# Gather and scatter by one-hot matmuls: the stationaries of line 717 take 125 columns instead of 128

## The chip, the cores and the metric

One core of a Trainium2 chip runs the kernel. The metric is device time in microseconds, the median of several executions: 469.66 us before the change, over 3 runs (468.04 to 470.31). One more execution was recorded by the hardware profiler; all rows of the trace are from that one.

## The reference

A block of a graph network on 1250 nodes with 512 features and 20000 edges. Everything is fp32.

```
xn  = layernorm(x)
gnn = relu(segsum((relu(segsum((xn @ W1.T + b1)[src], dst)) @ W2.T + b2)[src], dst))
q   = softmax(xn @ Wq.T, axis=-1) / sqrt(512);  k = softmax(xn @ Wk.T, axis=-2);  v = xn @ Wv.T
a   = q @ (k.T @ v) + xn
mix = a @ mW1.T @ mW2.T + a
x   = x + gnn + mix
x   = x + moe(layernorm(x))     # gates by 8 sinkhorn rounds, top 156 tokens for each of 8 experts
```

Here segsum(m, dst) adds the rows of m that have the same target node. The change lies in how this sum is prepared. The sum over edges is a product with the matrix A of edge counts: A[source, target] is how many edges lead from that source to that target. The kernel counts A once and uses it in both layers as a dense product.

## The kernel before

**Tiles.** The 1250 nodes are 10 tiles of 125 (TT = 125). The 512 features are 4 blocks of 128. The fp32 products are made of three terms, high by high, low by high and high by low part, and all are written by terms(), whose matmul is line 732: 12 matmuls of up to 512 columns for a tile, each with its own weight load.

**Counting the edges.** The edges are sorted by target and cut into 160 tiles of 125 edges (ET = 125). The targets are cut into 125 blocks of 8 to 11 (WIDTHS), and a visit is one pair of a block and an edge tile that may have edges into it: 322 visits in all. A visit is one matmul (line 717). Its stationary is a mark of 125 edges by 128 columns, with a 1 in the column that is the place of the source node within its tile of 125; its moving operand is a mark of 125 edges by 10 times the width of the block (80 to 110 columns), with a 1 in the column for the target and the tile of the source. The product adds the edge into the counts in a bank of PSUM, of which 125 rows are nodes.

**Who makes the marks.** VectorE makes both marks for four visits at a time (BATCH = 4): line 1683 the moving ones (RING_D, MARK_D), line 1685 the stationary ones (RING_S, MARK_S), the latter with 128 columns for each visit by comparing with every_home, which counts 0 to 127. A place in a tile is at most 124, so columns 125 to 127 hold only zeros. It then raises `marked`. The marks stand in a ring of 5 sets (2 sets at first), and a set is written again when `visited` says that TensorE has used it.

**Where the visits run.** They are put between the matmuls of other products. visits_in_products() gives each group of four visits a place: in the products vp, cp, q, x and h, six fp32 matmuls apart, or twelve in the products h. terms() calls visits() in front of its n-th matmul. The order on TensorE is so written out by hand; there is no scheduler. The first visit of a group waits for `marked`, and the last raises `visited`. When all visits into a bank are done, ScalarE copies 125 rows of it to AT (line 1300) and raises `adj_hi`, and the bank, one of two, is free for the next group of blocks.

**Other 16-bit products.** The rows further down also show lines 829 and 834 (a product of f16 stationaries of 125 columns, with 322 columns moving, between the fp32 matmuls of line 845), lines 1089 and 1090 (two bf16 stationaries of 125 columns, with 80 columns moving) and line 1039 (fp32 matmuls that fill waits of TensorE).

Of the kernel before, what the change touches and what calls it, by code (L numbers as in the profile page):

```python
# [33 lines left out]
TT = 125  # L34
# [11 lines left out]
BATCH = 4  # L46
# [178 lines left out]
def ring_slot(k):  # L225


    return k % RING_A if k < IN_A else RING_A + (k - IN_A) % RING_B
# [10 lines left out]
def gps_block(nc, x_in, src_t, dst_t, rows_in, gW1T, gb1, gW2T, gb2, WqT, WkT, Wv, mW1, mW2T,  # L239
# [5 lines left out]
    with ExitStack() as ctx:  # L245
# [170 lines left out]
        PS = [PSUM[:, 512 * b:512 * (b + 1)] for b in range(8)]  # L416

        def view(name, chunks=C):
            return PS[plan[name][0]].rearrange("p (c t) -> p c t", c=chunks)
# [50 lines left out]
        def hot_s(k):  # L470

            r = ring_slot(k)
            return MARK_S[0:ET, r] if r < RING_A else RING_S[0:ET, r - RING_A]

        def hot_d(k, w):

            r = ring_slot(k)
            return MARK_D[0:ET, r, :, 0:w] if r < RING_A else RING_D[0:ET, r - RING_A, :, 0:w]

        def width(b):  # L480

            return NT * WIDTHS[b]

        def group(g):

            lo, hi = GROUPS_OF_TARGETS[g]
            return EDGES[lo], EDGES[hi]
# [206 lines left out]
        def _(pe):  # L694
            def opens(name):

                for what, value in plan[name][2]:
                    pe.wait_ge(done[what], value)
                return PS[plan[name][0]]
# [4 lines left out]
            def visits(unit, n):  # L704

                for v in VISITS_AT.get((unit, n), ()):
                    b, s = ORDER[v]
                    g, k = GROUP_OF[b], v // BATCH
                    if s == 0 and b == GROUPS_OF_TARGETS[g][0]:
                        if g < 2:  # L710
                            opens(f"adj{4 + g}")
                        else:
                            pe.wait_ge(done["adj_hi"], g - 1)
                    if v % BATCH == 0:
                        pe.wait_ge(done["marked"], k + 1)
                    o = NT * (EDGES[b] - group(g)[0])
                    mm = pe.matmul(PS[4 + g % 2][:, o:o + width(b)], hot_s(k)[:, v % BATCH, :], hot_d(k, width(b))[:, v % BATCH, :],  # L717
                                   start=(s == 0), stop=(s == VISITS[b] - 1), skip_group_check=True)
                    if v % BATCH == BATCH - 1 or v == NV - 1:
                        mm.then_inc(done["visited"], 1)  # L720

            def terms(ps, stationary, moving, first=True, last=True, between=None, at=1, before=None, unit=None, base=0):

                pairs = [(a, b, c) for c in range(C) for a, b in ((0, 0), (0, 1), (1, 0))]
                for n, (a, b, c) in enumerate(pairs):
                    if n == at and between is not None:
                        between()
                    if n or not base:
                        visits(unit, base + n)
                    if n % 3 == 0 and before is not None:  # L730
                        before(c)
                    mm = pe.matmul(ps, stationary[a](c), moving[b](c), start=(first and n == 0), stop=(last and n == len(pairs) - 1))  # L732
                return mm
# [42 lines left out]
            for c in range(C):  # L776
                mm = pe.matmul(ps[0:TT, 0:NE], ones[:, 0:TT], gw1[:, c, :], start=(c == 0), stop=(c == C - 1))
# [18 lines left out]
            for c in range(C):  # L796
# [9 lines left out]
                if c == 0:  # L806
                    pe.wait_ge(done["kmax_step"], NT)
                    opens("kmt")
                    for f in range(C):
                        mm = pe.transpose(view("kmt")[:, f, 0:TT], KMAX[0:TT, 128 * f:128 * (f + 1)], ident[0:TT, 0:TT])  # L810
# [52 lines left out]
            for c in range(C):  # L863
                product(f"vp{c}", opens(f"vp{c}")[:], (block_of(WVH, c), block_of(WVL, c)), (rows_of(MPH), rows_of(MPL)),
                        unit=f"vp{c}")
                if c == 0:
                    pe.wait_ge(done["esum_step"], NT)
                    ps = opens("ks")
                    for f in range(C):
                        mm = pe.matmul(ps[:, f:f + 1], ESUM[0:TT, 128 * f:128 * (f + 1)], ones[0:TT, 0:1], start=True, stop=True)  # L870
# [9 lines left out]
            def mix(i):  # L880

                ps = opens(f"xq{i}")[0:TT, :]
                terms(ps, (tile_of(XTH, i), tile_of(XTL, i)), (rows_of(MPH), rows_of(MPL)), last=False, unit=f"x{i}")
                visits(f"x{i}", 12)
                pe.wait_ge(done["qtl_ready"], i + 1)
                if i == 0:
                    pe.wait_ge(done["cpl_ready"], C)
                    pe.wait_ge(done["cph_ready"], C)
                product(f"xq{i}", ps, (tile_of(QTH, i % 2), tile_of(QTL, i % 2)), (rows_of(CPH), rows_of(CPL)), first=False,
                        unit=f"x{i}", base=12)  # L890
# [53 lines left out]
            for ch, (c0, c1) in enumerate(CHUNKS):  # L944
                def place(f):
                    return PS[plan[f"z{ch}_{f}"][0]][:, 0:c1 - c0]
# [10 lines left out]
                with pe.If(large[0] > 0):  # L957
                    for k in range(NT):
                        pe.wait_ge(done["ac_ready"], ch * NT + k + 1)
                        for f in range(C):  # L960
                            for h in (H1H, H1L):
                                mm = pe.matmul(place(f), h[0:TT, k, 128 * f:128 * (f + 1)], AC[0:TT, k % 2, 0:c1 - c0], start=False, stop=False)
# [3 lines left out]
                for f in range(C):  # L966
                    k = NT - 1
# [97 lines left out]
            for name, lo, hi in (("key_a", 0, DVE_T), ("key_b", DVE_T, (DVE_T + NT) // 2), ("key_c", (DVE_T + NT) // 2, NT)):  # L1065
                ps = opens(name)
                for i in range(lo, hi):
                    if i % 4 == 0:
                        pe.wait_ge(done["p_ready"], SINKHORN + 1 + i // 4)
                    mm = pe.transpose(ps[:, TT * (i - lo):TT * (i - lo + 1)], WIDE[i // 4][0:TT, i % 4].rearrange("p e l -> p (e l)"),  # L1070
                                      ident[0:TT, 0:TT])
                closes(name, mm)
            for r in range(ROUNDS):
                ps = opens(f"rad{r}")
                p = NHI * (r // NHI)
                for n in range(p, r + 1):
                    if n == r:
                        pe.wait_ge(done["ind_ready"], r + 1)
                    mm = pe.matmul(ps[:, 0:1], same[:].rearrange("p e l -> p (e l)"), marks[:, n:n + 1], start=(n == p), stop=(n == r))
# [19 lines left out]
            for i in range(NT):  # L1099
# [3 lines left out]
                mm = pe.matmul(ps[0:SLOT, 0:NC], RS[h][0:TT, :, i - lo], PLACE[0:TT, :, i], start=(i == 0), stop=(i == NT - 1))  # L1103
# [4 lines left out]
            for i in range(NT):  # L1108
                h, lo = (0, 0) if i < MASKED[0][1] else (1, MASKED[1][0])
                mm = pe.matmul(ps[0:SLOT, 0:3 * NC], RS[h][0:TT, :, i - lo], GATE[0:TT, :, :, i], start=(i == 0), stop=(i == NT - 1))  # L1110
# [974 lines left out]
```

## Time and profile before

| | |
|---|---|
| median of 3 runs | 469.66 us (468.04 to 470.31) |
| the profiled execution | 469.05 us, of which the span from first to last instruction 467.3 us |
| TensorE matmuls busy | 449.9 us, 96% of the span, 2449 instructions |
| TensorE weight loads busy | 349.5 us, 75% |
| VectorE / ScalarE / GpSimd busy | 312.4 / 150.6 / 64.0 us |
| granted clock of TensorE, mean | 0.994 |
| visits (line 717) | 322, first at 87.5 us, last at 233.6 us |

PE is TensorE's matmul row, PEld its row of weight loads, DVE VectorE, ACT ScalarE. Matmuls are pipelined: the record of one begins when it is issued and ends when its last result has been written, by a model. So the records of neighbours overlap, and the time that a matmul costs is read from the distance of its start to the next start. Shapes stand as contraction*stationary columns, then the moving operand: `125*128 125x110 bf16` is a stationary of 125 rows and 128 columns and 110 moving columns.

### The profile page before, as it was taken

The numbers are of one execution on the slowest core, as the hardware profiler recorded it, in microseconds if no ns is written. First come the engines' busy times: TensorE is split into PE (matmuls) and PEld (weight loads), VectorE is DVE, ScalarE is ACT, GpSimd is POOL, SyncE is SP. The second block draws the span as 40 slices with busy tenths as digits, with TensorE's granted clock in tenths as the row PEclk, the third lists the DMA queues.
The fourth block names the chain that finished last, engine by engine and source line by source line (L and its number), as shares of the span: only waits on it lengthen the run. The fifth ranks groups of instructions, "written<-read, shape, count | busy, mean of one in ns | idle before, by whom it ended". The sixth has DMA issues, their size and how long they took to land.

```text
span 467.3 us, 6438 instructions
## 1 busy us (share of the span) xinstructions
PE 449.9 (96%) x2449; PEld 349.5 (75%) x2449; DVE 312.4 (67%) x681; ACT 150.6 (32%) x274; POOL 64.0 (14%) x108
## 2 busy tenths in 40 slices
PE   8999999999999999999999999999999999778995
PEld 4788778777777777777779999777777776454783
DVE  5995799899987888887741110444546567777972
ACT  4686454332322323242222111222141116441110
POOL 3188210000000000000004000004100000005642
PEclk9999999999999999999999999999999989999998
DMA  7902002912000000002100000004744459106791
GB/s 214 283 9 90 1 0 63 239 16 93 14 1 0 2 0 1 1 1 85 41 1 2 1 1 3 0 0 126 241 135 130 140 163 391 62 1 229 255 350 71
DMA packets 20824, 40.42 MB, mean 87 GB/s; under 512 B 2936, under 2 KB 3266, under 8 KB 20787
## 3 DMA queue, kind: packets, MB, share of 16 engines
q1 hardware_dynamic: 18547, 32.55, 22.4%
q0 software_dynamic: 2240, 7.39, 4.3%
q8 instruction: 23, 0.38, 0.3%
q14 instruction: 14, 0.11, 0.1%
HBM read 30.10 MB, written 10.30 MB: 86 GB/s over the span
## 4 chain that ended last, share of the span: by engine, by line
PE 85%; DVE 8%; ACT 3%; DMA 1%; issue 1%; SPq 1%; POOLq 0%; DVEq 0%; ACTq 0%
PE ps L732 47%; PE ps L1022 9%; PE ps L954 9%; PE ps L845 5%; PE ps L717 3%; PE ps L1039 2%; ACT scrap_a L1397 2%; PE ps L1148 2%; DMA RAW_K<-in_WkT 1%; PE ps L1118 1%; PE ps L877 1%; PE ps L981 1%; PE ps L766 1%; PE ps L1061 1%; PE ps L1003 1%
## 5 line engine op out<-in xcount | busy, mean ns | idle before, releaser
L1685 DVE TENSOR_TENSOR RING_S<-every_home,HOME 125x512 bf16<-125x512 f16 x64 | 43.8, 684 | 0.0
L954 PE MATMUL ps<-AT,H1H 125*128 125x416 f32 (+1 forms) x108 | 38.0, 352 | 0.0
L954 PE MATMUL ps<-AT,H1L 125*128 125x416 f32 (+1 forms) x108 | 38.0, 351 | 0.0
L1683 DVE TENSOR_TENSOR RING_D<-places,PLACES 125x440 bf16<-125x440 f16 (+3 forms) x64 | 36.4, 569 | 0.0
L1022 PE MATMUL ps<-H2H,AT 125*125 125x512 f32 x90 | 36.1, 402 | 0.0
L1022 PE MATMUL ps<-H2L,AT 125*125 125x512 f32 x90 | 35.5, 394 | 0.0
L1039 PE MATMUL ps<-WE0H 128*128 128x512 f32 x125 | 35.4, 419 | 0.0
L1753 DVE TENSOR_TENSOR ps<-ps,bias 125x512 f32<-125x512 f32 x20 | 14.0, 700 | 28.7 <-PE ps L732 28.7
L1834 DVE SCALAR_TENSOR_TENSOR ZL<-ps,ZH 128x416 fp32r<-128x416 f32 (+1 forms) x12 | 6.3, 584 | 38.7 <-ACT ZH L1350 38.7
L606 POOL TENSOR_TENSOR G2L<-RAW_G,G2H 128x512 fp32r<-128x512 f32 x4 | 5.0, 1299 | 188.4 <-ACT G2H L1167 188.4
L1039 PEld LDWEIGHTS ps<-WE0H 128*128 128x128 f32 x125 | 22.8, 197 | 3.7
L717 PEld LDWEIGHTS ps<-RING_D,RING_S 125*128 125x128 bf16 x254 | 14.0, 99 | 15.1 <-issue 10.5
L677 POOL DMA_INDIRECT YX<-scratch,idx x10 | 11.8, 1181 | 95.6 <-DVE idx L1990 92.9
L717 PE MATMUL ps<-RING_D,RING_S 125*128 125x110 bf16 (+3 forms) x254 | 22.6, 211 | 0.0
L1300 ACT ACTIVATE AT<-ps 125x440 fp32r<-125x440 f32 (+7 forms) x28 | 15.3, 545 | 18.7 <-PE ps L717 18.7
L954 PEld LDWEIGHTS ps<-AT,H1H 125*128 125x128 f32 x108 | 20.3, 188 | 0.2
L954 PEld LDWEIGHTS ps<-AT,H1L 125*128 125x128 f32 x108 | 20.3, 188 | 0.3
L1884 DVE SCALAR_TENSOR_TENSOR X<-ps,X 125x512 f32<-125x512 f32 x10 | 6.9, 692 | 19.7 <-PE ps L1034 19.7
L1022 PEld LDWEIGHTS ps<-H2H,AT 125*125 125x125 f32 x90 | 16.7, 186 | 4.0 <-issue 0.2
L1022 PEld LDWEIGHTS ps<-H2L,AT 125*125 125x125 f32 x90 | 16.7, 185 | 3.8
L732 PE MATMUL ps<-CPH,QTH 128*125 128x512 f32 x40 | 17.4, 435 | 0.0
L732 PE MATMUL ps<-WQH,XTH 128*125 128x512 f32 x40 | 17.4, 435 | 0.0
(401 smaller groups left out, 1175.6 us busy)
## 6 DMA issues: line engine op xcount, KB each, us to landing
RAW_E<-in_experts SPq DMA_DIRECT2D x8, 1024.0 KB, 9.2
RAW_AGAIN<-in_experts SPq DMA_DIRECT2D x3, 1024.0 KB, 8.8
X<-in_x SPq DMA_DIRECT2D x1, 2240.0 KB
out_x<-X SPq DMA_DIRECT2D x10, 224.0 KB
scratch<-X SPq DMA_DIRECT2D x10, 224.0 KB
scratch<-Y SPq DMA_DIRECT2D x10, 224.0 KB
RAW_K<-in_WkT SPq DMA_DIRECT2D x4, 256.0 KB, 5.1
RAW<-in_mW2T SPq DMA_DIRECT2D x1, 1024.0 KB, 12.8
```

What stands on the lines that cost most here:

```text
L677: nc.gpsimd.indirect_dma_start(out=YX[0:SLOT, j % RING].rearrange("p a f -> p (a f)"), out_offset=None, in_=scratch, in_offset=bass.Indire ...
L717: mm = pe.matmul(PS[4 + g % 2][:, o:o + width(b)], hot_s(k)[:, v % BATCH, :], hot_d(k, width(b))[:, v % BATCH, :], start=(s == 0), stop=(s ...
L732: mm = pe.matmul(ps, stationary[a](c), moving[b](c), start=(first and n == 0), stop=(last and n == len(pairs) - 1))
L845: mm = pe.matmul(ps[:], x[0:TT, i, f], e[0:TT, i % 4, :], start=(i == 0 and n == 0), stop=(i == NT - 1 and n == 2))
L954: pe.matmul(place(f), h[0:TT, k, 128 * f:128 * (f + 1)], AT[0:TT, k, c0:c1], start=(k == 0 and n == 0), stop=False)
L1022: pe.matmul(ps, AT[0:TT, k, t], h[0:TT, k, :], start=(k == 0 and n == 0), stop=False)
L1039: pe.matmul(PS[bank][:], WEH[0][:, 0, 0:128], WEH[0][:, 0, :], start=True, stop=True)
L1148: mm = pe.matmul(ps[p, 0:hi - lo], FTR[:, c, p], raw[q][:, c, lo:hi], start=(c == 0), stop=(c == C - 1), skip_group_check=True)
L1300: nc.scalar.activation(AT[0:TT, :, lo:hi], counts_of(g), ACT.Copy).then_inc(done["adj_hi"], 1)
L1683: V.tensor_tensor(hot_d(k, w), places[0:ET, 0:w].unsqueeze(1).broadcast_to([ET, BATCH, w]), PLACES[0:ET, c].unsqueeze(2).broadcast_to([ET, ...
L1685: V.tensor_tensor(hot_s(k), every_home[0:ET].unsqueeze(1).broadcast_to([ET, BATCH, 128]), HOME[0:ET, c].unsqueeze(2).broadcast_to([ET, BAT ...
L1753: V.tensor_tensor(ps, ps, bias[layer - 1][0:TT, :], ALU.add).then_inc(done["h1_biased" if layer == 1 else "h2_biased"], 1)
```

## The change

The stationary operand of each visit is cut to its first 125 columns, and the result goes to the first 125 rows of the bank. Only the slices in this one call are different.

```diff
-                    mm = pe.matmul(PS[4 + g % 2][:, o:o + width(b)], hot_s(k)[:, v % BATCH, :], hot_d(k, width(b))[:, v % BATCH, :],
+                    mm = pe.matmul(PS[4 + g % 2][0:TT, o:o + width(b)], hot_s(k)[:, v % BATCH, 0:TT], hot_d(k, width(b))[:, v % BATCH, :],
                                    start=(s == 0), stop=(s == VISITS[b] - 1), skip_group_check=True)
```

VectorE still makes marks of 128 columns, and no instruction is added, taken out or moved on any engine: 322 weight loads and 322 matmuls stand where they stood. The loads are of 125 columns, the matmuls write 125 rows, and the moving operand, the waits and the semaphores are the same. The columns that are left out held zeros, and the rows that are no longer written were not read.

## Rows read from the trace of the kernel before

**Rows 1.** windows: us; busy us (count) of each engine; granted clock, DMA share, GB/s.

```profile
85.00:235.00 150.00, 150.00 (x904) 111.99 (x903) 126.61 (x231) 47.33 (x91) 0.00 (x0) 1.00 0.12 35
```

**Rows 2.** chain of waits, 85 to 240 us: share by line.

```profile
by line: PE ps L732 85.7%; PE ps L717 10.3%; PE ps L877 2.8%; PE ps L845 0.9%; PE ps L870 0.5%
```

**Rows 3.** visits by shape: count, busy us, mean ns, idle before.

```profile
L717 PE MATMUL ps<-RING_D,RING_S 125*128 125x110 bf16 x140 | 13.6, 215 | 0.0
L717 PE MATMUL ps<-MARK_D,MARK_S 125*128 125x110 bf16 x49 | 4.7, 215 | 0.0
L717 PE MATMUL ps<-RING_D,RING_S 125*128 125x90 bf16 x48 | 4.3, 207 | 0.0
L717 PE MATMUL ps<-RING_D,RING_S 125*128 125x80 bf16 x46 | 3.9, 203 | 0.0
L717 PE MATMUL ps<-RING_D,RING_S 125*128 125x100 bf16 x20 | 1.9, 210 | 0.0
L717 PE MATMUL ps<-MARK_D,MARK_S 125*128 125x100 bf16 x12 | 1.2, 209 | 0.0
```

**Rows 4.** timeline of PE, one group of visits: start us, us.

```profile
128.15 0.40 PE L732 MATMUL ps<-WQH,XTL 128*125 128x512 f32 x1
128.39 0.38 PE L717 MATMUL ps<-RING_D,RING_S 125*128 125x110 bf16 x4
128.58 0.48 PE L732 MATMUL ps<-WQH,XTH 128*125 128x512 f32 x1
128.90 0.40 PE L732 MATMUL ps<-WQL,XTH 128*125 128x512 f32 x1
```

**Rows 5.** timeline of weight loads at the same place.

```profile
128.38 0.22 PEld L717 LDWEIGHTS ps<-RING_D,RING_S 125*128 125x128 bf16 x4 [0.28 <-issue]
128.55 0.19 PEld L732 LDWEIGHTS ps<-WQH,XTH 128*125 128x125 f32 x1
128.66 0.19 PEld L732 LDWEIGHTS ps<-WQL,XTH 128*125 128x125 f32 x1
```

**Rows 6.** line 717, first visit of that group alone: min/median/max ns.

```profile
L717 PE MATMUL ps<-RING_D,RING_S x1: 223/223/223, 128.4 to 128.4; 125*128 125x110 bf16 x1
```

**Rows 7.** line 717, all: min/median/max ns; idle us, times before its loads.

```profile
L717 PEld LDWEIGHTS ps<-RING_D,RING_S x254: 95/98/111, 116.5 to 233.6; 125*128 125x128 bf16 x127
L717 PE MATMUL ps<-RING_D,RING_S x254: 197/212/226, 116.5 to 233.6; 125*128 125x110 bf16 x70, 125*128 125x90 bf16 x24, 125*128 125x80 bf16 x23, 125*128 125x100 bf16 x10
  issue: 14.8, 54
  DVE RING_S L1685: 4.5, 16
```

**Rows 8.** timeline of PE, groups of 100 and 80 columns.

```profile
98.22 0.35 PE L717 MATMUL ps<-MARK_D,MARK_S 125*128 125x100 bf16 x4
...
158.02 0.32 PE L717 MATMUL ps<-RING_D,RING_S 125*128 125x80 bf16 x4
```

**Rows 9.** timeline, 16-bit stationaries of 125 columns back to back.

```profile
415.95 0.13 PEld L1089 LDWEIGHTS ps<-before,ones 125*125 125x125 bf16 x1 [1.04 <-DVE before L1947]
415.95 0.25 PE L1089 MATMUL ps<-before,ones 125*125 125x80 bf16 x1 [0.61 <-DVE before L1947]
416.00 0.14 PEld L1090 LDWEIGHTS ps<-equal,tri 125*125 125x125 bf16 x1
416.03 0.23 PE L1090 MATMUL ps<-equal,tri 125*125 125x80 bf16 x1
416.06 0.19 PEld L1039 LDWEIGHTS ps<-WE0H 128*128 128x128 f32 x1
```

**Rows 10.** timeline, a 16-bit 125-column load behind an fp32 product.

```profile
76.55 0.39 PE L845 MATMUL ps<-EH,XNL 125*128 125x512 f32 x1
76.78 0.44 PE L829 MATMUL ps<-SEL,keys 80*125 80x322 f16 x2
...
76.55 0.36 PEld L829 LDWEIGHTS ps<-SEL,keys 80*125 80x125 f16 x2
```

## The prediction

> **What bounds the kernel now.** [...] The chain of waits over the same stretch consists of TensorE alone: 85.7% is line 732, the fp32 products, and 10.3% line 717, the visits [rows 2]. No other engine ends a wait in it. Time that a visit gains or loses is therefore gained or lost by the kernel, almost one for one: nothing in this stage has slack to take it, and what comes after starts from it.
>
> A busy matmul row says nothing of how close together the matmuls run, since records overlap: 322 visits with records of some 0.21 us [rows 3, 7] would be 68 us one after the other, and the chain gives them 10.3% of 155, 16 us. What counts is the distance from one start to the next. In a group of four visits of 110 columns [rows 4] the last fp32 matmul starts at 128.15, the visits at 128.39, the fp32 product goes on at 128.58, its second matmul starts at 128.90. The weight loads of the same place are the second view [rows 5]: four loads of 128 bf16 columns from 128.38, then the fp32 loads at 128.55 and 128.66.
>
> Two things are to be seen there. First, the first visit's load does not run under the fp32 matmul before it: the load engine stands for 0.28 us ("issue") and starts only 0.01 before the visit itself. This happens in front of 54 + 16 = 70 groups [rows 7]; 16 name VectorE's marks, but the distance is the same, so I count them alike (the other 11 of the 81 groups have no such idle before them). The visit then waits in the array for its weights, and its record shows it: 0.223 us [rows 6] against a median of 0.212 [rows 7], 0.011 late. Second, the other loads are hidden under the visit before them.
>
> **What changes.** 322 weight loads take 125 bf16 columns instead of 128; the instructions and their order, the moving columns, every wait, VectorE's marks and ScalarE's copies stay as they are. The copies read 125 rows before and after. So three terms are possible: how long a load takes, how close visits follow each other, and what the first load of a group costs.
>
> *The load itself.* A load of 128 bf16 columns has a record of 0.098 us [rows 7]. The trace has 16-bit loads of 125 columns too: 0.13 and 0.14 for bf16 [rows 9]. Three columns fewer, yet 0.037 longer. [...] Loads hold the path only where they are not hidden, so the 0.037 is not simply multiplied by 322.
>
> *Distance between visits.* Now: a group of four of 110 columns spans 0.38 us [rows 4]; less the last record (0.212) and the 0.011 by which the first is late, 0.157 for three distances, 0.052 each. 100 columns: 0.35 less 0.207 and 0.011, 0.044. 80 columns: 0.32 less 0.200 and 0.011, 0.036 [rows 8]. The records of the shapes are the means [rows 3] less the first visits' share of the lateness. 90 columns I put between, at 0.040. The distance follows the columns, so the moving data set it, not the load. With 125 columns the load may set it. Its pace is seen where such loads stand back to back [rows 9]: loads at 415.95, 416.00 and 416.06, 0.055 apart, with matmuls of 80 columns between them. I take 0.056 for every shape. Ends: 0.050, the shorter of the two distances there, and 0.060, the longer. The shapes count 189 of 110 columns, 32 of 100, 46 of 80 [rows 3] and the remaining 55 of 90; three in four have a visit behind them in their group. Added: 142 x 0.004 + 24 x 0.012 + 41 x 0.016 + 34.5 x 0.020 = 0.57 + 0.29 + 0.66 + 0.69 = 2.2 us. With 0.050 (110 columns stay at their own 0.052) it is 1.0, with 0.060 3.2.
>
> *First load of a group.* Here the change may even help. A 16-bit load of 125 columns behind an fp32 matmul stands in [rows 10]: it starts at 76.55 together with that matmul, and the 16-bit matmul follows at 76.78, 0.23 later, with its weights in place. The fast load of the visits never does that behind an fp32 product of line 732: all 70 stand back. If the ordinary load is the one that may go early, a first visit starts streaming 0.23 after the last fp32 matmul, where now it takes 0.24 + 0.011. Read to 0.01, that saves 0.01 to 0.02; I take 0.017, in 70 groups 1.2 us (ends 0.7 and 1.4). It needs the marks 0.23 earlier; if the 16 groups that name VectorE cannot have them, they lose 0.04 each instead and the term shrinks to about 0.3.
>
> *Last visit to fp32.* The fp32 load starts with the last visit and takes 0.11 (128.55 to 128.66) [rows 5], before as after: nothing. [...]
>
> Sum: +2.2 - 1.2 = +1.0 us, ends -0.4 (1.0 - 1.4) and +2.9 (3.2 - 0.3). The profiled execution took 469.05 us (its span 467.3), so 470.1 by itself; the median of the three runs before is 469.66, 0.6 higher, and the forecast for a median is **470.7 us**.
>
> **Rivals.**
>
> *A: the first load stays behind the fp32 matmul.* Place: the step from line 732 to line 717, 70 times. For: all 70 stand back now, and the kind of matmul in flight could be the reason rather than the kind of load; the one place of the other sort [rows 10] has 80 rows and f16. Against: that place has the same fp32 matmul in front. Price: the load is exposed in full. The first matmul and its load start together and its record is 0.25 instead of 0.20 [rows 9], 0.053 late rather than 0.011; 70 x 0.042 = 2.9 more and no 1.2 saved: +2.2 + 2.9 = +5.1, 474.8 us. Each group that stays back moves the sum by 0.042 + 0.017, so from 1.0 us it passes 2.35 at 23 of the 70 groups; below that the answer is still no change.
>
> *B: the ordinary load is as slow as an fp32 load.* fp32 loads of 125 columns are 0.11 apart where they bind [rows 5]. Distance 0.11: 142 x 0.058 + 24 x 0.066 + 41 x 0.070 + 34.5 x 0.074 = 15.3, less 1.2: +14.1, 483.8 us. Against it: 0.055 [rows 9], and records of 0.13 to 0.14 for 16-bit against 0.19 for fp32. [...]
>
> *C: faster.* The first load goes under the fp32 matmul and the distance stays with the moving columns: -1.2, 468.5 us. It decides when the distance for 110 columns stays at 0.052 and the others stay under it by their present margin. Against: 0.055 with only 80 columns moving.
>
> *D: nothing happens.* The load is made as before although three columns are left out, so 469.7. Against: 0.13 and 0.14 for 125 bf16 columns in this very program.
>
> **Chances and range.** Forecast 58%, A 24%, B 4%, C 7%, D 7%. What can be told from no change here is about 0.5%, 2.35 us: below 467.3 or above 472.0. Slower takes A, B and the uppermost part of the forecast's own spread (72.6 less 72.0 at its end), 5%: 33%. Faster: C stays within the 2.35, only the scatter of the runs (468.04 to 470.31) could carry it over: 5%. The rest, 62%, is no change. The range must reach A, since A alone is a quarter: low 468.6 (C), high 475.4 (A with its distance at 0.058).
>
> **What would show it.** Loads of line 717 with a record of 0.13 to 0.14 (else D). The four matmuls of a group at equal distances, 0.055 to 0.057, whatever their columns. The "issue" idle of 14.8 us before the loads gone and the first visit's load starting with the fp32 matmul before it; if it is still there and the first records are some 0.25 to 0.26 us, A is right. A distance of 0.1 would be B. Prediction and sum fail together if time moves outside 85 to 235 us.

## The result and the profile after

| | before | after |
|---|---|---|
| median (22 runs each) | 468.25 us (467.11 to 470.31) | 469.64 us (468.51 to 473.56) |
| ratio after / before | | 1.0034, 95% interval 1.0019 to 1.0049 |
| profiled execution | 469.05 us, span 467.3 | 472.16 us, span 470.4 |

The kernel became slower by a third of a per cent, 1.6 us (0.9 to 2.3). That is small and still clear of zero. Behind it are two effects of opposite sign, one of them larger than the sum and the other nearly as large.

The stretch from 85 to 235 us is filled by TensorE as before [rows 1, 2]: first the windows view (busy time and count of PE, PEld, DVE, ACT, POOL, then clock, DMA share, GB/s), then the shares of the chain of waits by line.

```profile
85.00:235.00 150.00, 150.00 (x898) 122.08 (x898) 126.60 (x232) 46.99 (x90) 0.00 (x0) 1.00 0.13 36
```

```profile
by line: PE ps L732 83.1%; PE ps L717 11.6%; PE ps L877 2.8%; PE ps L845 2.1%; PE ps L870 0.5%; PE ps L860 0.1%
```

The load row is busy for 122.08 us instead of 111.99, and the visits hold 11.6% of the chain instead of 10.3%. All loads of line 717 have a median record of 0.138 us now, against 0.098 [rows 7] (below, a load with the short record is called fast, one with the long record ordinary), and the list of what ended the idle time before them, which named "issue" 54 times and the marks 16 times, is empty:

```profile
L717 PEld LDWEIGHTS ps<-RING_D,RING_S x254: 134/138/139, 118.5 to 236.7; 125*125 125x125 bf16 x127
L717 PE MATMUL ps<-RING_D,RING_S x254: 199/222/242, 118.8 to 236.8; 125*125 125x110 bf16 x70, 125*125 125x90 bf16 x24, 125*125 125x80 bf16 x23, 125*125 125x100 bf16 x10
its engine sat idle before it (us, times) until:
who waited for it (us, times):
```

A group of 110 columns in the timeline of matmuls, and below it one of 80, to be held against [rows 4, 8]:

```profile
149.90 0.39 PE L732 MATMUL ps<-CPH,QTL 128*125 128x512 f32 x1
150.13 0.39 PE L717 MATMUL ps<-RING_D,RING_S 125*125 125x110 bf16 x4
150.33 0.47 PE L732 MATMUL ps<-WQH,XTH 128*125 128x512 f32 x1
150.64 0.39 PE L732 MATMUL ps<-WQL,XTH 128*125 128x512 f32 x1
...
160.58 0.37 PE L717 MATMUL ps<-RING_D,RING_S 125*125 125x80 bf16 x4
```

and its weight loads, against [rows 5]:

```profile
149.90 0.48 PEld L717 LDWEIGHTS ps<-RING_D,RING_S 125*125 125x125 bf16 x4
150.31 0.19 PEld L732 LDWEIGHTS ps<-WQH,XTH 128*125 128x125 f32 x1
150.41 0.19 PEld L732 LDWEIGHTS ps<-WQL,XTH 128*125 128x125 f32 x1
```

The first load of the group starts at 149.90, together with the fp32 matmul before it; in [rows 5] it started 0.01 before its own matmul. The first visit follows 0.23 after the fp32 matmul with its weights in place. In exchange the group is longer: 0.39 less a record of 0.212 leaves 0.178 for three distances, 0.059 each (0.052 before), and with 80 columns 0.37 less 0.200 leaves 0.17, 0.057 each (0.036 before). The distance no longer follows the moving columns, with 0.059 and 0.057 for 110 and 80 of them; that the load sets it is the reading that the experiments try.

Now the same over all groups. A visit whose load started only 0.01 before it has a longer record (0.223 us for the first visit of [rows 6] against the 0.212 of an undisturbed one), so what its record is longer than an undisturbed one of its shape is added to its start. The 241 distances inside groups then sum to 11.19 us before and 14.07 after (0.0464 and 0.0584 on average; after, visits of 80, 90, 100 and 110 columns all stand 0.058 behind one of their own shape), +2.9 us. From the fp32 matmul to the streaming of the first visit, the 70 places behind a product of line 732 take 0.248 us each before and 0.230 after, together -1.3 us. The visits begin and end here, in the kernel before and after:

```profile
87.53 0.38 PE L717 MATMUL ps<-MARK_D,MARK_S 125*128 125x110 bf16 x4
...
233.54 0.27 PE L717 MATMUL ps<-RING_D,RING_S 125*128 125x110 bf16 x2
```

```profile
89.44 0.39 PE L717 MATMUL ps<-MARK_D,MARK_S 125*125 125x110 bf16 x4
...
236.74 0.26 PE L717 MATMUL ps<-RING_D,RING_S 125*125 125x110 bf16 x2
```

146.01 us from the first group to the last before, 147.30 after: +1.29 us, 1.0028 of the whole, inside the measured interval. (The two effects give +1.6; the rest of the stretch came out 0.3 shorter, 0.2 of it in the step from the last visit of a group to the fp32 product.) But the visits also begin 1.9 us later, at 89.44. The windows view of the first 20 us, before and then after, shows one difference: the mean granted clock is 1.00 and 0.91 (0.50 in the stretch from 11 to 14 us of the kernel after).

```profile
0.00:20.00 20.00, 17.34 (x75) 10.99 (x76) 14.19 (x38) 10.33 (x19) 6.11 (x37) 1.00 0.91 228
```

```profile
0.00:20.00 20.00, 16.32 (x64) 10.61 (x65) 12.69 (x36) 8.63 (x17) 6.12 (x37) 0.91 0.91 237
```

Ahead of it, TensorE waited for the DMA transfer of the gate weights, in the timelines before and after:

```profile
8.04 1.04 PE L777 MATMUL ps<-gw,onesr 128*125 128x8 f32 x8 [0.24 <-DMA gw<-in_gate]
```

```profile
9.31 1.04 PE L777 MATMUL ps<-gw,onesr 128*125 128x8 f32 x8 [1.61 <-DMA gw<-in_gate]
...
11.92 0.63 PE L732 MATMUL ps<-WKL,XTH 128*125 128x512 f32 x1
```

The wait was 1.61 instead of 0.24 us, and then the fp32 matmuls ran for a while at a granted clock of 0.50, with records of 0.63 instead of 0.39 and starts 0.43 apart instead of 0.23. All this lies over 75 us ahead of the first changed instruction. Whether it belongs to the change is asked below.

### The profile page after: what moved, and what is told of

Same layout as the page of the kernel before. It is cut to its first block, busy times and chain, and to the rows that moved or that the text cites. A ratio compares the mean times of both kernels' runs of the same rounds, so it can differ in the third digit from the quotient of the medians.

```text
span 470.4 us, 6438 instructions
## 1 busy us (share of the span) xinstructions
PE 452.0 (96%) x2449; PEld 361.8 (77%) x2449; DVE 312.3 (66%) x681; ACT 150.6 (32%) x274; POOL 64.1 (14%) x108
## 4 chain that ended last, share of the span: by engine, by line
PE 86%; DVE 7%; ACT 3%; issue 1%; DMA 1%; SPq 1%; POOLq 0%; DVEq 0%; ACTq 0%
PE ps L732 47%; PE ps L1022 9%; PE ps L954 9%; PE ps L845 5%; PE ps L717 4%; PE ps L1039 2%; ACT scrap_a L1397 2%; PE ps L1148 2%; DMA gw<-in_gate 1%; PE ps L1118 1%; PE ps L877 1%; PE ps L766 1%; PE ps L981 1%; PE ps L1061 1%; PE ps L1003 1%
## 5 line engine op out<-in xcount | busy, mean ns | idle before, releaser
L717 PEld LDWEIGHTS ps<-RING_D,RING_S 125*125 125x125 bf16 x254 | 24.4, 137 | 7.6
L717 PE MATMUL ps<-RING_D,RING_S 125*125 125x110 bf16 (+3 forms) x254 | 24.4, 220 | 0.0
L732 PE MATMUL ps<-MPH,XTH 128*125 128x512 f32 x40 | 17.4, 435 | 0.0
```

What stands on the lines that cost most here:

```text
L717: mm = pe.matmul(PS[4 + g % 2][0:TT, o:o + width(b)], hot_s(k)[:, v % BATCH, 0:TT], hot_d(k, width(b))[:, v % BATCH, :], start=(s == 0), s ...
```

## The experiments

The theory: (1) a stationary of other than 128 bf16 columns is loaded the ordinary way (0.138 us at 125 columns in the trace above), and at 125 columns such loads stand about 0.058 us apart; (2) an ordinary load may start under the fp32 matmul in front of it (70 of 70 in the changed kernel), the fast one may not (0 of 70 in the kernel before). The rivals are that (2) has another reason, and that (1) is not the load's columns. All kernels set the number of columns in the same place; in the kernel before plus these lines, the calls stand at line 718 and the fp32 products at 733:

```diff
+                    w = TT if v % BATCH == 0 else 128        # first125
-                    mm = pe.matmul(PS[4 + g % 2][:, o:o + width(b)], hot_s(k)[:, v % BATCH, :], ...
+                    mm = pe.matmul(PS[4 + g % 2][0:w, o:o + width(b)], hot_s(k)[:, v % BATCH, 0:w], ...
```

**First visit alone (first125).** 125 columns in the first visit of a group, 128 in the other three, as in the diff above.

> Only the first visit of each group of four takes 125 columns and writes 125 rows; the other three take 128. Theory (two opposite effects: an ordinary load may start under the fp32 matmul in front, a fast one may not; and an ordinary load of 125 columns sets the distance between visits at 0.058 us): only the first effect is left. The loads of the 70 first visits start 0.23 us before their matmul, their distance to the fp32 matmul falls by 0.018 us, the distances inside a group stay at 0.036 to 0.051: -1.3 us, ratio 0.997, faster than both kernels. Rival (what lets the load start early is that all visits of the group are of one kind, or the change of kind inside a group costs as much as the other does): the second visit is late by about 0.01 to 0.04 us, and the sum is 0 to +2 us.

Measured: 467.33 us against 468.89, ratio 0.997 (0.9946 to 0.9993). Matmuls and loads of one group:

```profile
148.76 0.39 PE L733 MATMUL ps<-WQH,XTL 128*125 128x512 f32 x1
148.99 0.36 PE L718 MATMUL ps<-RING_D,RING_S 125*125 125x110 bf16 x4
149.17 0.48 PE L733 MATMUL ps<-WQH,XTH 128*125 128x512 f32 x1
```

```profile
148.76 0.43 PEld L718 LDWEIGHTS ps<-RING_D,RING_S 125*125 125x125 bf16 x4
149.14 0.19 PEld L733 LDWEIGHTS ps<-WQH,XTH 128*125 128x125 f32 x1
```

The first load starts with the fp32 matmul (148.76), as 67 of the 70 do (for the other three VectorE finished the marks too late, and they start 0.03 to 0.25 after the fp32 matmul, each 0.12 behind its marks), the first visit 0.23 after it, and the group takes 0.36: less 0.212, 0.049 for each distance. So this kernel has the early first load of the changed kernel and the short distances of the kernel before. The groups run from 87.60 to 232.37, 144.77 us, 1.24 less than before:

```profile
87.60 0.36 PE L718 MATMUL ps<-MARK_D,MARK_S 125*125 125x110 bf16 x4
...
232.37 0.25 PE L718 MATMUL ps<-RING_D,RING_S 125*125 125x110 bf16 x2
```

The theory holds, and this version is ahead of both kernels.

**The other three (rest125).**

```diff
+                    w = 128 if v % BATCH == 0 else TT
```

> The mirror image: the first visit of each group takes 128 columns, the other three 125. Theory: the fast load of the first visit stands back behind the fp32 matmul as before (idle of about 0.28 us in front of 70 loads, record 0.223), and the distances are 0.058: the loss of 2.9 us without the 1.3 saved, ratio 1.006. Rival (the early start has nothing to do with the kind of the first load): the first load goes early here too, +1.6 us, ratio 1.0034 as in the changed kernel.

Measured: 471.55 us against 468.89, ratio 1.0057 (1.0037 to 1.0077).

```profile
149.97 0.40 PE L733 MATMUL ps<-WQH,XTL 128*125 128x512 f32 x1
150.21 0.40 PE L718 MATMUL ps<-RING_D,RING_S 125*128 125x110 bf16 x4
150.42 0.48 PE L733 MATMUL ps<-WQH,XTH 128*125 128x512 f32 x1
```

```profile
149.74 0.18 PEld L733 LDWEIGHTS ps<-WQH,XTL 128*125 128x125 f32 x1
150.20 0.27 PEld L718 LDWEIGHTS ps<-RING_D,RING_S 125*128 125x128 bf16 x4 [0.28 <-issue]
```

The load of the first visit has its 0.28 us of idle back, in front of 70 groups again, and stands 0.23 behind the fp32 matmul; the distances are long, 0.0584 on average. Groups from 87.22 to 236.27: 149.05 us, +3.04. So it is the kind of the first load that decides whether it goes early: this kernel and the changed one differ only in the columns of the first visit, loaded and written.

**127 columns (all127).**

```diff
+                    w = 127
```

> Every visit takes 127 columns. Theory (the fast load exists for exactly 128 columns): records of about 0.138 us, first loads early, distances 0.059, together +0.2 us over the changed kernel: ratio 1.004. Rival (the cost follows the number of columns smoothly, or depends on 125 in another way): somewhere between the two kernels, with loads of 0.098 us.

Measured: 471.17 us against 468.89, ratio 1.0054 (1.0033 to 1.0075).

```profile
L718 PEld LDWEIGHTS ps<-RING_D,RING_S 125*127 125x127 bf16 x254 | 24.6, 138 | 7.5
L718 PEld LDWEIGHTS ps<-MARK_D,MARK_S 125*127 125x127 bf16 x68 | 6.6, 139 | 2.1
```

With a single column fewer than 128 the load is an ordinary one: the mean record is 0.138 us, where 128 columns had a median of 0.098 [rows 7]. The distances average 0.0592 us. The first load starts with the fp32 matmul in all 70 places. Groups from 87.40 to 234.59, 147.19 us, +1.18, where +1.5 was expected, since the first visits start 0.227 behind the fp32 matmul and not 0.230. The ratio, from six runs, lies higher than this stretch alone gives (1.0025). Most of the difference goes with the clock: five of the six had a mean granted clock of 0.988, median 471.20 us, and the four runs of the kernel before at 0.988 or 0.989 have a median of 470.26, so that like against like it is +0.9 us; the sixth, at 0.994, took 470.07, 1.8 above the median of the other 13 of before (468.30). With so few runs the stretch is the better measure.

**64 columns (all64).**

```diff
+                    w = 64
```

> Every visit takes 64 columns and writes 64 rows; the counts of the sources with place 64 to 124 in their tile are left out, so only the time is read. [...] Rival (the distance of 0.058 us is a fixed price of the ordinary load and not of its columns): distances stay at 0.058, +1.6 us, ratio 1.0034.

Measured: 487.26 us against 468.89, ratio 1.0398 (1.0373 to 1.0424). That is far above the 1.0034 of the rival.

```profile
150.00 0.40 PE L733 MATMUL ps<-MPH,XTL 128*125 128x512 f32 x1
150.32 0.39 PE L718 MATMUL ps<-RING_D,RING_S 125*64 125x110 bf16 x4
150.64 0.49 PE L733 MATMUL ps<-MPH,XTH 128*125 128x512 f32 x1
150.98 0.39 PE L733 MATMUL ps<-MPL,XTH 128*125 128x512 f32 x1
```

```profile
150.32 0.24 PEld L718 LDWEIGHTS ps<-RING_D,RING_S 125*64 125x64 bf16 x4 [0.37 <-DVE RING_S L1686]
150.64 0.18 PEld L733 LDWEIGHTS ps<-MPH,XTH 128*125 128x125 f32 x1
```

Inside the group the distances are short again: the 241 sum to 11.17 us, against 11.19 in the kernel before and 14.07 in the changed one. So the 0.058 is not a fixed price that comes with every stationary of other than 128 columns, and the rival is out. But each change of kind costs: the first visit starts 0.32 after the fp32 matmul instead of 0.23 and its load only with it, and the fp32 matmul starts 0.32 after the first visit instead of 0.19 [rows 4]. Over the 70 places it is 0.350 on average from the fp32 matmul to the streaming of the first visit (0.248 before), and 0.474 from the last visit to the second fp32 matmul (0.344 before): 70 x 0.102 + 81 x 0.130 = 17.7 us. The other 11 groups, behind fp32 transposes and one matmul of one column, pay about as much going in (0.12 on average), 1.3 us. The stretch of the groups is 164.95 us, +18.94, which these terms make up. What in the change to and from 64 columns costs this time no run here shows. The idle row names VectorE's marks here, and so it did in 16 of the 70 cases before [rows 7]; with 63 other groups under "issue" at the same idle time the name is that of the last event, not a cause.

**96 columns (all96).**

```diff
+                    w = 96
```

> Every visit takes 96 columns and writes 96 rows; the counts of the sources with place 96 to 124 in their tile are left out, so only the time is read. [...]

Measured: 466.91 us against 468.16, ratio 0.9973 (0.995 to 0.9996).

```profile
148.11 0.39 PE L733 MATMUL ps<-WQH,XTL 128*125 128x512 f32 x1
148.33 0.36 PE L718 MATMUL ps<-RING_D,RING_S 125*96 125x110 bf16 x4
148.51 0.48 PE L733 MATMUL ps<-WQH,XTH 128*125 128x512 f32 x1
```

```profile
148.11 0.45 PEld L718 LDWEIGHTS ps<-RING_D,RING_S 125*96 125x96 bf16 x4
148.49 0.19 PEld L733 LDWEIGHTS ps<-WQH,XTH 128*125 128x125 f32 x1
```

The question was whether the price seen with 64 columns, 0.102 us going in and 0.130 coming back, is there with 96 as well. It is not: the load starts with the fp32 matmul, the visit 0.22 later, and from the last visit to the second fp32 matmul it is 0.343 on average (0.344 before). The distances are 0.045 us where 80, 90 or 100 columns move and 0.051 with 110. Together with 0.058 for 125 columns and 0.059 for 127 this makes 0.0134 us for 29 columns, 0.46 ns each at a granted clock of 1.00 in the stretch: an estimate from three widths. By that slope a load of 64 columns would need 0.030 us (0.045 less 32 times 0.46 ns), less than the 0.036 at which visits of 80 moving columns stood in the kernel before, which agrees with the short distances of all64. The stretch is 145.11 us, 0.90 less than before. The price at the change seen with 64 columns thus ends somewhere between 64 and 96 columns; at which number was not tried.

**Both again (after_again, first125_again).** The changed kernel and the kernel with only the first visit at 125, unchanged.

> The changed kernel once more, beside the others on the same chip. Theory: +1.6 us in the visits and nothing elsewhere, ratio 1.0034; the stretch from the first to the last visit takes 147.35 us against 146.07 of the kernel before. Its first profiled execution had one stretch of 3.4 us at half clock at 10 us that the kernel before had not; if that comes and goes from run to run it is no effect of the change (rival: it stands here again, and part of the measured loss is the clock).

Measured: 469.68 us against 468.16, ratio 1.0033 (1.0013 to 1.0052). The groups in the new trace:

```profile
87.01 0.39 PE L717 MATMUL ps<-MARK_D,MARK_S 125*125 125x110 bf16 x4
...
234.31 0.26 PE L717 MATMUL ps<-RING_D,RING_S 125*125 125x110 bf16 x2
```

147.30 us once more, to 0.01. They begin at 87.01, not at 89.44, and the first 20 us have a granted clock of 1.00:

```profile
0.00:20.00 20.00, 17.11 (x77) 11.24 (x78) 15.19 (x39) 10.38 (x19) 6.12 (x37) 1.00 0.93 225
```

The late transfer and the slow clock at the start are therefore not something that the change always brings. The spread of the runs goes with the clock: of the 22 of the changed kernel the seven with a mean clock of 0.990 or less are the seven slowest, 471.12 to 473.56 us; the other fifteen, at 0.994 to 1.0, took 468.51 to 470.52. The kernel before has such runs too: the six of its 29 beside this one with 0.991 or less are its slowest, 469.94 to 471.56. Without these runs on either side, 7 of the changed kernel have a median of 469.28 and 23 of the kernel before 468.07, +1.2 us, which is what the stretch of the groups gives (+1.29). The changed kernel had a low clock somewhat more often, in 12 of 34 runs against 10 of 46; whether by chance is not shown, and the part of the 1.6 us beyond the stretch may come from there.

> The kernel with 125 columns in the first visit of each group only, once more, for a closer interval and a second trace. Theory: first visits start 0.230 us after the fp32 matmul, distances as in the kernel before, stretch of the visits 144.8 us, ratio 0.997. Rival (its first result was scatter): ratio 0.999 to 1.001 at an unchanged stretch.

Measured: 467.38 us against 468.16, ratio 0.998 (0.9956 to 1.0004). The groups run from 87.33 to 232.10, 144.77 us as in its first trace:

```profile
87.33 0.36 PE L718 MATMUL ps<-MARK_D,MARK_S 125*125 125x110 bf16 x4
...
232.10 0.26 PE L718 MATMUL ps<-RING_D,RING_S 125*125 125x110 bf16 x2
```

The gain of 1.24 us in the stretch repeats to 0.01; in total time one of the two intervals lies wholly below 1, the other reaches 1.0004. The two ratios make it a gain of 0.2 to 0.3%, and 1.24 us are 0.26%.

## Why the prediction was right

*What bounds.* Right: the stretch from 85 to 235 us stayed TensorE's alone, busy for 150.00 us before and after at a granted clock of 1.00, and what the visits lost arrived at the end. +1.29 us there, 1.0034 in total.

*The load itself.* Right: 0.134 to 0.139 us for all 322 against the forecast 0.13 to 0.14. The evidence was the two loads of 125 columns in [rows 9]; that 127 columns have the long record too, 0.138 us, only all127 showed. Rival D is out.

*Distance between visits.* That the load sets the distance was right (0.045 us at 96 columns, 0.058 at 125, 0.059 at 127), the size a little low: 0.058 for each shape against the 0.056 taken, within the ends of 0.050 and 0.060. The term measured +2.9 us, not +2.2. It was read from the starts of three loads [rows 9], 0.05 and 0.06 apart at a resolution of 0.01, and the third of them is an fp32 load (line 1039), so only one distance was between ordinary bf16 loads. Read the way the distances of before were, with the lateness of the records in, the same rows give 0.06: the two matmuls of 80 columns end at 416.20 and 416.26. 241 times 0.002 is 0.5 of the missing 0.7, the rest is rounding, in the distances before and in this one. Reading a term of 241 distances from one place was the weak step.

*First load.* Right in kind and size: 70 of 70 went early, 0.230 after the fp32 matmul, -1.3 us against -1.2. The evidence was a single place with f16 and 80 rows, and it carried over to bf16 and 125 rows. Rival A, which gave it a quarter of the chance, is out by the changed kernel's own trace, and rest125 shows its premise the other way round: with a fast load in front, the idle stays. The marks were never late for the earlier load; the 16 groups that name VectorE went early too.

*Last visit to fp32.* Nothing, as forecast, to 0.2 us in sum. Writing 125 rows of the bank instead of 128 has no term either: in first125, where the first visits write 125, the 241 distances sum to 11.18 us against 11.19 before.

*The sum.* +1.0 us forecast, +1.3 in the stretch and +1.6 (0.9 to 2.3) by the ratio. The median given for the kernel, 470.7, started from 469.66, the median of three runs; over 22 runs that of before is 468.25. The sum was added to a base that stood 1.4 us too high, more than the error of the sum, and the two errors have opposite signs: the forecast is 1.1 us above the measured 469.64. The stated range, 468.6 to 475.4, would have held rival A as well; what decides between the two is the trace, not the time.

*Rivals B and C.* B (0.11 per load) is out by 0.058. C would have needed distances that follow the moving columns; all96 nearly has that, and is 0.9 us shorter there.

## What to carry to other kernels

Give a bf16 stationary 128 columns where such matmuls follow each other closely and move few columns (here up to the 110 of the widest visit, 0.051 us apart behind fast loads and 0.058 behind ordinary ones; by the slope from 0.036 at 80 moving columns to 0.051 at 110, an estimate, up to about 125). Give it fewer (96, 125 and 127 were tried, and 64 was costly) where a lone or first bf16 matmul follows an fp32 one of 512 columns, because there the ordinary load started with the fp32 matmul and the fast one did not, 0.230 against 0.248 us to the streaming of the first visit. Look at the first matmul of a run and at the others separately: one setting for all 322 visits hid 1.3 us of gain under 2.9 us of loss. When the expected effect is half a per cent, compare the stretch in the traces (147.30 twice, 144.77 twice) and not the totals, which a clock change elsewhere moves by more.

## What the runs showed of the hardware

- A load of 128 bf16 columns never started under an fp32 product of line 732 (70 of 70 in the kernel before, 70 in rest125), but did under bf16 visits (in the kernel before all 241 later loads of the groups started 0.001 to 0.012 us after the visit in front), and 0.001 to 0.002 us after the start of the matmul in front in the 11 groups behind the fp32 transposes (10) and a matmul of one column (1). A load of 96, 125 or 127 columns started 2 to 4 ns after the start of the fp32 matmul wherever its marks were ready: 70 of 70 in the changed kernel and with 127 columns, 67 of 70 with 96 columns. Which property of the matmul in flight holds the fast load back was not tried.
- Stationaries of 64 columns between fp32 matmuls of 125 to 128 cost 0.10 us going in and 0.13 coming back, 19 us over 81 groups; with 96 columns nothing (0.227 us going in, 0.343 coming back, against 0.248 and 0.344 before).
- One execution of the changed kernel reached its first visit 1.9 us later than the kernel before, the next one 0.5 us earlier (87.01 against 87.53). In the late one TensorE had stood idle for 1.61 us at the gate weights and then ran at a granted clock of 0.50 from 11 to 14 us; in the two others the idle time was 0.24 and 0.36 us and the granted clock 1.00 over the first 20 us. So much comes from outside of what is compared.
